# A two-layer graph network on one core: the ranks by the second sort digit as per-partition running counts on VectorE

## The chip, the cores and the metric

The kernel runs on one core of a Trainium2 chip (trn2). The time is device microseconds of one execution; lower is better. TensorE is called PE here, VectorE DVE, ScalarE ACT, GpSimd POOL and the queue of the sync engine SP, as in the profile.

## The reference, cut to what matters

```python
# x: 3125 x 256, 50000 edges (src, dst), sorted by dst before the kernel sees them
for i in range(3):                                     # layer 0, three hops
    msg = H[src] * edge_weight[:, None]
    Hn = segment_sum(msg, dst, 3125) @ Wn[i].T + bn[i]
    H = Hn + H @ Ws[i].T + bs[i]
    if i != 2: H = elu(H)
x = layernorm(x + H)
# layer 1: graph attention with 8 heads of 32 over the same edges
h = x @ W.T
alpha = leaky_relu(a_src.h[src] + a_dst.h[dst] + relu(edge_attr @ edge_W.T + edge_b).h[dst])
attn = softmax of alpha over the edges of each dst
out = layernorm(x + segment_sum(h[src] * attn, dst) + bias)
```

What counts here is how the edges are brought into order on the chip. The kernel doesn't use that they arrive sorted: it sorts records of 8 floats (source, destination, weight, three attributes, a flag) twice, once by pairs of node windows and once by destination.

## The kernel before, in words

The work goes through these stages, in order of time in the profiled execution.

**Ranks and scatter by pair, to about 559 us.** DVE and PE rank the 128 x 392 records by pair of windows, and POOL writes them to rows of memory, one indirect DMA for each of the 392 columns (line 608). SP reads the result back as `recs_pair`.

**Ranks by the low digit, on DVE and PE, in the shadow of that scatter.** The sort by destination is a radix sort with two digits of 64 values: the low six bits first, then the bits above. `digit_ranks(0)` (PE lines 753 to 778, DVE lines 1417 to 1470) computes the ranks. The 392 columns form 14 groups (`SEGS`) of 28 (`SEGC`). In a first pass DVE builds a one-hot of the digit for 7 groups at a time (128 x 448 bf16, line 1411) and PE sums all of them with a matrix of ones (line 757, 56 matmuls of 448 columns). DVE makes first ranks of the totals (lines 1426 to 1438, a scan of 896 elements and the starts of the digits) and PE loads them into two banks of PSUM as `seed` (line 762). In a second pass, for each of 28 columns and each half, DVE builds the one-hot again, PE adds the triangle of ones (`below_b`, line 770), DVE multiplies the bank by the one-hot and reduces (lines 1451 and 1454) to read the rank, and PE adds the rest of the ones (`rest_b`, line 776). Every fourth column DVE turns 56 ranks of each partition into row numbers in four small instructions (lines 1462 to 1468) and counts up `s_place`. Four slots of one-hots (`oh`) turn. Between these steps PE does the first products with the weights.

**Adjacency blocks, 573 to about 1100 us.** Steps of eight chunks build dense blocks of 128 x 256 of the weighted adjacency matrix and store them in memory. Meanwhile POOL scatters the records by the low digit (line 618) and reads them back to `rec` (line 627), at 1126 us.

**Three hops, 1105 to about 2128 us.** Hop `k` goes through 7 groups `g` of 512 node columns (the last has 53). In a group, PE starts with 8 records of line 915 and then, for each of 25 windows `w`, multiplies the loaded block `a_t` with two halves of the table (line 923, four records in the trace for two instructions). SP loads `a_t` ten ahead (lines 525 and 528). `behind` puts small products of the next hop after some windows (line 794), from `w` = 8 on; the first of them waits for `s_ht`, the ELU of the group before, which ACT and DVE make (DVE lines 1659 and 1663). The layer norm of the last hop and the projection follow in hop 2 in the same way.

**The second digit, inside hop `k` = 1.** `digit_ranks(1)` is run again by PE and DVE, cut into steps by generators. After each window of hop 1 PE issues the next of its rank steps, by the function `issued`: two a window for the first 28 windows (the counts), then one a window (seeds, `below_b` and `rest_b`), 172 steps in all:

```python
if k == 1:
    slot = g * USED + w
    for _ in range(issued(slot + 1) - issued(slot)):
        next(side)
```

DVE issues the steps that belong to a group's 25 windows (line 1651) ahead of that group's ELU. The DVE's pass is paced by PE's matmuls through `s_drd` and `s_pre`, and PE waits for DVE through `s_doh`, `s_dseed` and `s_pick`. As the places of four columns of all 14 groups are ready (56 DMAs), POOL scatters them to `rows_dst` (line 633, 392 indirect DMAs in all) and reads the sorted records back (line 638). `split_features` on DVE in the last group of hop 2 (line 1620) waits for that read.

**The attention layer, to the end.** POOL gathers the rows of `h` by edge (line 647, 416 indirect DMAs), PE and DVE compute the scores, and a second pass sums the messages.

The sort must keep the order of equal digits: the ranks of the second digit go over the columns first and over the partitions within a column, which is the order in which line 1468 with stride 392 laid out the records by the low digit (rank `r` in partition `r & 127`, column `r >> 7`).

Of the kernel before, what the change touches and what calls it, by code (L numbers as in the profile page):

```python
# [13 lines left out]
P = 128  # L14
# [42 lines left out]
HN = HS * DIG  # L57

# [18 lines left out]
assert USED <= 1 << WBITS and 4 * WBITS <= 24  # L77
assert EC % PIECE == 0 and PIECE % 4 == 0 and 0 < LAST < EC and EC % U == 0 and SEGS * SEGC == EC and SEGS % 2 == 0 and SEGC % MID == 0
# [4 lines left out]
def build(nc, x, src, dst, edge_attr, edge_weight, Wn, bn, Ws, bs, W, a_src, a_dst, edge_W, edge_b, bias, out):  # L83
    with ExitStack() as ctx:
# [63 lines left out]
        summed, q = carve(q, [DIG, SEGS])  # L148

# [93 lines left out]
        window_row = picked[0:1, :, :, :].rearrange("p b g s -> p (b g s)")[:, 0:2 * NC].rearrange("p (r c) -> p r c", r=2)  # L243
# [341 lines left out]
        def _(pool):  # L585
# [94 lines left out]
        SLOTS2 = SEGC  # L680
        RANK_OPS = 2 * SEGC + 2 + 4 * SEGC + 2

        def issued(slot):
            return min(2 * min(slot, SLOTS2) + max(0, slot - SLOTS2), RANK_OPS)

# [4 lines left out]
        def _(pe):  # L690
# [62 lines left out]
            def digit_ranks(q):  # L753
                n0 = 4 * SEGC * q
# [83 lines left out]
            for n, _ in enumerate(digit_ranks(0)):  # L838
# [63 lines left out]
            def hop(k, g):  # L902
# [14 lines left out]
                for w in range(USED):  # L917
# [347 lines left out]
        def _(dve):  # L1265
# [151 lines left out]
            def digit_ranks(q, stride, to, begins, d):  # L1417

                n0 = 4 * SEGC * q
                m0 = 2 * SEGC * q  # L1420
# [21 lines left out]
                for i in range(SEGC):  # L1442
# [14 lines left out]
                    if i % MID == MID - 1:  # L1457
                        j = i // MID
                        part = slice(i + 1 - MID, i + 1)
                        e = d + 16 + 3 * j  # L1460
                        dve.wait_ge(s_rk, m0 + 2 * i + 2)
                        v.tensor_copy(rk_i[:, 0, :, :], rk.rearrange("p (s i) -> p s i", s=SEGS)[:, :, part]).then_inc(s_dg, 1)
                        dve.wait_ge(s_dg, e + 1)
                        v.tensor_scalar(rk_i[:, 1, :, :], rk_i[:, 0, :, :], P - 1, None, ALU.bitwise_and).then_inc(s_dg, 1)
                        v.tensor_scalar(rk_i[:, 2, :, :], rk_i[:, 0, :, :], SHIFT, None,
                                        ALU.logical_shift_right).then_inc(s_dg, 1)
                        dve.wait_ge(s_dg, e + 3)
                        v.scalar_tensor_tensor(out=place[:, to, :].rearrange("p (s i) -> p s i", s=SEGS)[:, :, part],  # L1468
                                               in0=rk_i[:, 1, :, :], scalar=float(stride), in1=rk_i[:, 2, :, :],
# [3 lines left out]
            LOW_END = LOW0 + 16 + 3 * SEGC // MID  # L1473
# [35 lines left out]
            for _ in digit_ranks(0, EC, 1, low_begins, LOW0):  # L1509
# [84 lines left out]
            def dst_ranks():  # L1594
# [5 lines left out]
                yield from digit_ranks(1, NCD, 0, window_begins, DST0)  # L1600
                yield
                dve.wait_ge(s_ex, 1)
                v.tensor_copy(ex_col[:, :], bank[6][0:HI, 0:1]).then_inc(s_exc, 1)
                dve.wait_ge(s_exc, 1)
                v.tensor_scalar(started[:, :], iota_f[0:HI, 0:NC], ex_col[:, 0:1], None, ALU.is_ge).then_inc(s_exc, 1)
                yield
                dve.wait_ge(s_ex, 2)
                v.tensor_scalar(window_row[:, 0, :], bank[7][0:1, 0:NC], -1.0, None, ALU.add).then_inc(s_exc, 1)
                of = [window_row[:, 0, :].rearrange("p (g j) -> p j g", j=4)[:, j, :] for j in range(4)]
                word = window_row[:, 1, :].rearrange("p (j g) -> p j g", j=4)  # L1610
                for j, (high, low, to) in enumerate(((of[3], of[2], word[:, 0, :]), (word[:, 0, :], of[1], word[:, 1, :]),
                                                     (word[:, 1, :], of[0], quad_windows[:, :]))):
                    dve.wait_ge(s_exc, j + 3)
                    v.scalar_tensor_tensor(out=to, in0=high, scalar=float(1 << WBITS), in1=low, op0=ALU.mult,
                                           op1=ALU.add).then_inc(s_exc, 1)
# [27 lines left out]
            for k in range(HOPS):  # L1643
                for g in range(NG):
# [4 lines left out]
                    if k == 1:  # L1649
                        for _ in range(issued((g + 1) * USED) - issued(g * USED)):  # L1650
                            next(side)
                        if g == NG - 1:
                            next(side, None)
# [294 lines left out]
```

## Time and profile before

| | us |
|---|---|
| Median of 3 runs | 3014.15 (3014.09 to 3016.46) |
| The profiled execution, its own time | 3018.76 |
| Its span in the trace | 3016.7 |
| PE busy (share of the span) | 2460.3 (82%) |
| POOL busy | 1855.6 (62%) |
| DVE busy | 1722.3 (57%) |
| ACT busy | 1073.7 (36%) |
| Mean granted TensorE clock | 0.923 |

Shares of busy time are means over stages with different limits. Here each stage is bounded by another engine, so the stretch that the change touches has to be read by itself. A matmul in fp32 shows as two records in the trace.

### The profile page before, as it was taken

To read this page: it belongs to the slowest core of one execution; us is meant where nothing else is said; L and a number is where in the kernel's file an instruction comes from. 1 tells how busy PE (TensorE), PEld (TensorE's weight loads), DVE (VectorE), ACT (ScalarE), POOL (GpSimd) and SP (SyncE) were. 2 spreads that over 40 slices of the span, in tenths; PEclk is the share of its full clock that TensorE was granted. 3 is DMA by queue.
4 is the path that set the end of the run, shared out by engine and by line. 5 is a ranking of instruction groups with operands and counts; after the bars stand their busy time and mean duration, and the time that the engine had idled before them with its cause. 6 is when DMAs were issued, how large, how long until landed. Compare 5 with 4: busy or idle time off the path is not lost.

```text
span 3016.7 us, 48565 instructions
## 1 busy us (share of the span) xinstructions
PE 2460.3 (82%) x9398; PEld 1569.3 (52%) x9399; DVE 1722.3 (57%) x4280; ACT 1073.7 (36%) x3018; POOL 1855.6 (62%) x1739
## 2 busy tenths in 40 slices
PE   6999976477777779999899999999776767738883
PEld 5888853255555544445444454445554545525552
DVE  7765558799999940001334411103777777766667
ACT  1222221398888840000000000000333333338773
POOL 4777777777777770000057777770577777757774
PEclk9999979699999999999999999999788888869997
DMA  4000000255555565443344444543477777747772
GB/s 128 3 4 3 3 25 3 99 183 183 184 184 184 184 196 152 129 132 110 101 122 121 128 115 128 143 134 106 141 217 218 218 217 218 217 132 230 215 212 85
DMA packets 425652, 415.45 MB, mean 138 GB/s; under 512 B 85386, under 2 KB 411489, under 8 KB 424929
## 3 DMA queue, kind: packets, MB, share of 16 engines
q1 hardware_dynamic: 367681, 348.28, 36.9%
q0 software_dynamic: 57888, 66.23, 9.4%
q8 instruction: 32, 0.52, 0.1%
q14 instruction: 51, 0.42, 0.0%
HBM read 247.08 MB, written 167.17 MB: 137 GB/s over the span
## 4 chain that ended last, share of the span: by engine, by line
PE 37%; POOL 23%; issue 15%; SPq 10%; DVE 6%; DMA 4%; DVEq 3%; ACT 1%; ACTq 0%; POOLq 0%
PE psum L923 27%; POOL rows_by_pair L608 13%; POOL gath L647 10%; SPq L497 7%; PE psum L1039 2%; PE psum L915 2%; DMA gath<-gat_rows,rec 2%; SPq L491 2%; PE psum L794 1%; DMA adjacency<-merged 1%; PE psum L883 1%; PE psum L853 1%; DVE acc L1848 1%; DVEq L414 1%; DVE x L1848 1%
## 5 line engine op out<-in xcount | busy, mean ns | idle before, releaser
L633 POOL DMA_INDIRECT rows_by_dst<-rec,place x392 | 382.6, 976 | 534.0 <-DVE place L1468 405.9
L923 PE MATMUL psum<-a_t,acc 128*128 128x512 f32 (+1 forms) x1400 | 553.7, 551 | 0.0
L647 POOL DMA_INDIRECT gath<-gat_rows,rec x416 | 404.6, 973 | 213.0 <-issue 117.1
L618 POOL DMA_INDIRECT rows_by_low_digit<-rec,place x392 | 437.6, 1116 | 127.7 <-issue 127.7
L853 PE MATMUL psum<-rhot,lw 128*128 128x256 f32 x1440 | 381.8, 419 | 162.7 <-ACT lw L1110 124.3
L608 POOL DMA_INDIRECT rows_by_pair<-rec,place x392 | 389.0, 992 | 159.5 <-issue 126.7
L853 PEld LDWEIGHTS psum<-rhot,lw 128*128 128x128 f32 x1440 | 276.4, 206 | 268.1 <-ACT lw L1110 170.7
L923 PEld LDWEIGHTS psum<-a_t,acc 128*128 128x128 f32 x1400 | 257.3, 195 | 272.1 <-issue 268.3
L1576 DVE SCALAR_TENSOR_TENSOR merged<-merged,same_of,psum 128x256 f32<-128x256 f32 x720 | 309.7, 476 | 30.4 <-PE psum L853 18.7
L923 PE MATMUL psum<-a_t,x 128*128 128x512 f32 (+1 forms) x700 | 294.3, 549 | 0.0
L1110 ACT ACTIVATE lw<-lhot,recs_pair 128x128 f32<-128x128 bf16 x720 | 236.8, 387 | 98.6 <-DVE lhot L1559 87.8
L994 PE MATMUL psum<-x,acc 128*128 x832 | 258.5, 458 | 5.1 <-DVE acc L1715 4.4
L1039 PE MATMUL psum<-ht 128*128 128x264 f32 x832 | 214.2, 402 | 48.8 <-DVE acc L1848 45.2
L663 POOL TENSOR_TENSOR ht<-gath,digits 128x1024 f32<-128x1024 f32 x104 | 198.7, 1914 | 64.9 <-PE psum L1039 56.8
L1039 PEld LDWEIGHTS psum<-ht 128*128 128x128 f32 x832 | 151.1, 191 | 111.9 <-DVE acc L1848 86.0
L735 PEld LDWEIGHTS psum<-table,ohhiT 32*128 32x128 f32 x784 | 181.1, 318 | 53.2 <-issue 33.7
L994 PEld LDWEIGHTS psum<-x,acc 128*128 128x128 f32 x832 | 180.0, 231 | 50.6 <-issue 16.9
L735 PE MATMUL psum<-table,ohhiT 32*128 32x16 f32 x784 | 202.2, 375 | 1.4 <-issue 1.2
L1659 DVE TENSOR_SCALAR et<-et 128x512 f32<-128x512 f32 (+1 forms) x28 | 11.0, 394 | 334.0 <-ACT et L1138 333.8
L1715 DVE TENSOR_TENSOR acc<-wT,psum 128x528 f32<-128x528 f32 x208 | 145.2, 698 | 94.7 <-issue 41.8
L923 PEld LDWEIGHTS psum<-a_t,x 128*128 128x128 f32 x700 | 126.2, 191 | 114.0 <-issue 109.0
L1345 DVE SCALAR_TENSOR_TENSOR terms<-psum,kst,earlier 128x128 f32<-128x128 f32 (+1 forms) x392 | 139.8, 412 | 44.8 <-PE psum L720 34.3
(322 smaller groups left out, 3392.9 us busy)
## 6 DMA issues: line engine op xcount, KB each, us to landing
a_t<-adjacency SPq DMA_DIRECT2D x450, 256.0 KB, 2.7
adjacency<-merged SPq DMA_DIRECT2D x721, 128.0 KB
gat_h_by_edge<-gath SPq DMA_DIRECT2D x104, 528.0 KB, 4.2
gath<-gat_h_by_edge SPq DMA_DIRECT2D x104, 528.0 KB, 3.9
gath<-gat_rows,rec POOLq DMA_INDIRECT x416
rows_by_pair<-rec,place POOLq DMA_INDIRECT x392
rows_by_low_digit<-rec,place POOLq DMA_INDIRECT x392
rows_by_dst<-rec,place POOLq DMA_INDIRECT x392
```

Of the source, the lines that this page charges most:

```text
L497: sp.dma_start(adj[bass.ds(to[j], 1), :, :].rearrange("b p c -> p (b c)"), merged[:, j, :]).then_inc(s_st[j], 16)
L608: pool.indirect_dma_start(out=rows_pair, in_=rec[:, c, :], out_offset=bass.IndirectOffsetOnAxis(ap=place[:, 0, c:c + 1], axis=0), in_offse ...
L618: pool.indirect_dma_start(out=rows_low, in_=rec[:, c, :], out_offset=bass.IndirectOffsetOnAxis(ap=place[:, 1, c:c + 1], axis=0), in_offset ...
L633: pool.indirect_dma_start(out=rows_dst, in_=rec[:, c, :], out_offset=bass.IndirectOffsetOnAxis(ap=place[:, 0, c:c + 1], axis=0), in_offset ...
L647: pool.indirect_dma_start(out=gath[:, g % 4, c % 4, :], out_offset=None, in_=hh_dram, in_offset=bass.IndirectOffsetOnAxis(ap=rec_i[:, c, 0 ...
L735: pe.matmul(bank[7 * s][:, j * LO:(j + 1) * LO], ohhiT[:, 4 * s + j, :], table[:, half, :], start=True, stop=True, skip_group_check=True). ...
L853: pe.matmul(bank[j % 4][:, 0:SW], lw[:, p, j, :], rhot[:, p, j, :], start=True, stop=True).then_inc(s_bmm, 1)
L923: i = pe.matmul(sums[b], table_g[:, w, b * P:(b + 1) * P], a_t[:, q % NA, 0:width(g)], start=False, stop=w == USED - 1)
L994: i = pe.matmul(bank[4 + j][:, 0:HX], ohT[:, q % 2, j * P:(j + 1) * P], x0[:, bass.ds(ws[4 * (q % 2) + j], 1), :].rearrange("p c k -> p (c ...
L1039: pe.matmul(bank[4 * (q % 2) + j][:, 0:HX], onehot[:, q // 2, 4 * (q % 2) + j, :], val[:, q, j, :], start=True, stop=True).then_inc(s_mm, 1)
L1110: nc.scalar.activation(lw[:, p, j, :], lhot[:, p, j, :], ACT.Copy, scale=recs_pair[:, bass.ds(at, 1), 2]).then_inc(s_lw, 1)
L1576: v.scalar_tensor_tensor(out=merged[:, j, :], in0=merged[:, (j - 2) % U, :], scalar=same_of[:, bass.ds(s, 1)], in1=bank[j % 4][:, 0:SW], o ...
```

## The change

The layout of the records by the low digit is another one, and the ranks by the second digit are computed in another way. The 392 columns now form 7 groups (`RUNS`) of 56 (`RUN`). The order of the records goes over the groups, then the partitions, then the columns in a group: rank `r` lies in run `r // 56`, partition `run & 127`, group `run >> 7`. For that the low digit's row number takes nine small DVE instructions for every four columns instead of four.

For the second digit DVE counts the one-hots of each partition by itself: a bf16 sum (`counts`) over the 56 columns of all 7 groups at once. PE then runs two matmuls on these counts, one with ones (totals) and one with `below_b` (the partitions below). DVE keeps the next rank of each digit in `first` (128 x 448 fp32): a step multiplies it by the one-hot, adds the one-hot to it, and reduces the product to the ranks. PE has three side steps left in hop 1, at window 0 of groups 1, 2 and 3. DVE issues 55, 21, 20 and 16 steps ahead of the ELUs of groups 0 to 3, and none after. The window starts (lines 1603 to 1614) are computed inside the third and fourth of these parts. POOL scatters in batches of 28 DMAs in place of 56; there are 392 as before. The seeds, the 56 count matmuls, the 56 `below_b` and the 56 `rest_b` matmuls of the second digit are gone; those of the low digit stay.

```diff
+RUNS = HS
+RUN = EC // RUNS
...
+        first = seed[:, 0, :, :]
+        counts = seed[:, 1, :, :].rearrange("p s d -> p (s d)")[:, 0:HN // 2].bitcast(BF16).rearrange("p (s d) -> p s d", d=DIG)
...
-            for j in range(SEGC // MID):
+            for j in range(RUN // MID):
                 pool.wait_ge(s_place, SEGC // MID + j + 1)
                 for i in range(MID):
-                    for s in range(SEGS):
-                        c = s * SEGC + j * MID + i
+                    for s in range(RUNS):
+                        c = s * RUN + j * MID + i
...
+        RANK_STEPS = [RUN - 1, 1 + 20, 20, RUN - 40, 0, 0, 0]
...
             def dst_windows():
-                yield from digit_ranks(1)
+                pe.wait_ge(s_drd, 4 * SEGC + RUN - 1)
+                pe.matmul(bank[6][:, 0:HN], ones_b[:, :], flat(counts), start=True, stop=True).then_inc(s_pre, 1)
+                pe.matmul(bank[7][:, 0:HN], below_b[:, :], flat(counts), start=True, stop=True).then_inc(s_pre, 1)
+                yield
+                pe.wait_ge(s_dseed, 3)
                 pe.transpose(bank[6][0:HI, 0:P], begin[:, 2, HI:2 * HI], identf[:, :]).then_inc(s_ex, 1)
...
-                    if k == 1:
-                        slot = g * USED + w
-                        for _ in range(issued(slot + 1) - issued(slot)):
-                            next(side)
+                    if k == 1 and w == 0 and g in (1, 2, 3):
+                        next(side)
...
+                        v.tensor_scalar(eighth, rank_, 3, None, ALU.logical_shift_right).then_inc(s_dg, 1)
...
+                        v.tensor_scalar(run_, eighth, 0.5, 8.0 / RUN, ALU.add, ALU.mult).then_inc(s_dg, 1)
...
+                        v.scalar_tensor_tensor(out=eighth, in0=run_, scalar=RUN / 8.0, in1=eighth, op0=ALU.mult,
+                                               op1=ALU.is_gt).then_inc(s_dg, 1)
...
+                onehot_of(0, counts)
+                onehot_of(1, oh[:, 1, :, :])
+                for i in range(1, RUN):
+                    if i + 1 < RUN:
+                        if i >= 4:
+                            dve.wait_ge(s_drd, used + i - 3)
+                        onehot_of(i + 1, oh[:, (i + 1) % 4, :, :])
+                    dve.wait_ge(s_doh, built + i + 1)
+                    if i > 1:
+                        dve.wait_ge(s_drd, used + i - 1)
+                    v.tensor_tensor(counts, counts, oh[:, i % 4, :, :], ALU.add).then_inc(s_drd, 1)
+                    yield
...
+                v.tensor_tensor_scan(flat(run_sums), flat(run_keep), flat(run_totals), 0.0, ALU.mult, ALU.add).then_inc(s_dg, 1)
...
+                v.tensor_tensor(first, first, bank[7][:, 0:HN].rearrange("p (s d) -> p s d", d=DIG), ALU.add).then_inc(s_dseed, 1)
...
+                    v.tensor_tensor(picked[:, i % 2, :, :], first, oh[:, i % 4, :, :], ALU.mult).then_inc(s_pick, 1)
+                    dve.wait_ge(s_pick, picks + i + 1)
+                    v.tensor_tensor(first, first, oh[:, i % 4, :, :], ALU.add).then_inc(s_drd, 1)
+                    v.tensor_reduce(rk.rearrange("p (s i) -> p s i", s=RUNS)[:, :, i], picked[:, i % 2, :, :], X,
+                                    ALU.add).then_inc(s_rk, 1)
...
                     if k == 1:
-                        for _ in range(issued((g + 1) * USED) - issued(g * USED)):
+                        for _ in range(RANK_STEPS[g]):
                             next(side)
```

## Rows read from the trace of the kernel before

**Rows 1.** The page, chain that ended last: shares of the span by line.
```profile
PE psum L923 27%; POOL rows_by_pair L608 13%; POOL gath L647 10%; SPq L497 7%; PE psum L1039 2%; PE psum L915 2%; DMA gath<-gat_rows,rec 2%; SPq L491 2%; PE psum L794 1%; DMA adjacency<-merged 1%; PE psum L883 1%; PE psum L853 1%; DVE acc L1848 1%; DVEq L414 1%; DVE x L1848 1%
```

**Rows 2.** Windows of hop 0, hop 1 and its group 1: busy times, clock, DMA.
```profile
1105.00:1418.60 313.60, 313.51 (x853) 154.56 (x854) 13.10 (x26) 23.48 (x48) 15.06 (x16) 0.99 0.47 137
1418.60:1775.10 356.50, 348.56 (x1033) 172.07 (x1032) 136.46 (x305) 24.76 (x53) 182.77 (x187) 0.99 0.42 115
...
1475.30:1541.90 66.60, 58.66 (x156) 27.64 (x155) 29.10 (x61) 3.72 (x9) 7.03 (x7) 0.92 0.35 99
```

**Rows 3.** The chain in order of time, starts of groups: start us, us, what.
```profile
1303.55 3.43 PE psum L915 x8
...
1353.35 3.43 PE psum L915 x8
1356.79 15.45 PE psum L923 x36
...
1418.61 3.50 PE psum L915 x8
...
1475.34 3.43 PE psum L915 x8
...
1541.95 3.43 PE psum L915 x8
1596.48 3.43 PE psum L915 x8
...
1775.11 3.50 PE psum L915 x8
...
1822.39 3.43 PE psum L915 x8
```

**Rows 4.** Groups of instructions in hop 1, forms kept apart.
```profile
L633 POOL DMA_INDIRECT rows_by_dst<-rec,place x188 | 183.8, 978 | 465.6 <-DVE place L1468 405.9 <-issue 59.7
...
L1411 DVE TENSOR_TENSOR digits<-digits,iota_b 128x448 bf16<-128x448 bf16 x112 | 38.5, 386 | 34.3 <-PE psum L757 34.2
```

**Rows 5.** Timeline of hop 1: first one-hots, then the seeds.
```profile
1420.97 1.30 DVE L1411 TENSOR_TENSOR digits<-digits,iota_b 128x448 bf16<-128x448 bf16 x4
...
1485.10 1.70 DVE L1426 COPY digits<-psum 128x448 f32<-128x448 f32 x2 [3.69 <-PE psum L757]
...
1494.71 1.86 PE L762 MATMUL psum<-digits,identf 128*128 128x448 f32 x2 [7.94 <-DVE digits L1438]
...
1496.37 3.26 PE L923 MATMUL psum<-a_t,x 128*128 128x512 f32 x4
```

**Rows 6.** Timeline of DVE, low digit's second pass and the wait behind it.
```profile
461.06 0.61 DVE L1451 TENSOR_TENSOR digits<-psum,digits 128x448 f32<-128x448 f32 x1
461.71 0.62 DVE L1454 TENSOR_REDUCE digits<-digits 128x7 f32<-128x448 f32 x1
462.25 0.68 DVE L1411 TENSOR_TENSOR digits<-digits,iota_b 128x448 bf16<-128x448 bf16 x2
...
479.58 0.19 DVE L1462 CAST digits<-digits 128x56 int32<-128x56 f32 x1
...
480.26 0.69 DVE L1411 TENSOR_TENSOR digits<-digits,iota_b 128x448 bf16<-128x448 bf16 x2
...
569.35 0.81 DVE L1545 TENSOR_SCALAR low_i<-recs_pair 128x720 int32<-128x720 int32 x1 [10.27 <-DMA recs_pair<-rows_by_pair]
```

**Rows 7.** Timeline of DVE, the ELU of group 1 of hop 1.
```profile
1542.52 0.43 DVE L1659 TENSOR_SCALAR et<-et 128x512 f32<-128x512 f32 x1 [3.06 <-ACT et L1138]
...
1544.26 1.29 DVE L1663 SCALAR_TENSOR_TENSOR ht<-zt,et 128x512 f32<-128x512 f32 x2 [0.73 <-ACT zt L1140]
```

**Rows 8.** Timeline, second scatter: its start, its read-back, and its reader.
```profile
1532.91 1.21 POOL L633 DMA_INDIRECT rows_by_dst<-rec,place  x1 [405.89 <-DVE place L1468]
...
2046.11 0.57 POOL L638 DMA_DIRECT2D rec<-rows_by_dst  x1 [2.52 <-DMA rows_by_dst<-rec,place]
...
2102.97 1.05 DVE L1620 COPY digits<-rec 128x1728 f32<-128x1728 f32 x1
```

More of the change, by code:

```diff
@@ L837, in _ @@
             products = first_products()
-            for n, _ in enumerate(digit_ranks(0)):
+            for n, _ in enumerate(digit_ranks()):
                 if n % 3 == 2:
@@ L1459, in digit_ranks @@
                         part = slice(i + 1 - MID, i + 1)
-                        e = d + 16 + 3 * j
+                        e = d + 16 + 8 * j
+                        rank_, eighth, run_ = (rk_i[:, a, :, :] for a in range(3))
                         dve.wait_ge(s_rk, m0 + 2 * i + 2)
-                        v.tensor_copy(rk_i[:, 0, :, :], rk.rearrange("p (s i) -> p s i", s=SEGS)[:, :, part]).then_inc(s_dg, 1)
+                        v.tensor_copy(rank_, rk.rearrange("p (s i) -> p s i", s=SEGS)[:, :, part]).then_inc(s_dg, 1)
@@ new lines, in digit_ranks @@
+                        dve.wait_ge(s_dg, e + 4)
+                        v.scalar_tensor_tensor(out=run_, in0=eighth, scalar=-1.0, in1=run_, op0=ALU.mult,
+                                               op1=ALU.add).then_inc(s_dg, 1)
+                        dve.wait_ge(s_dg, e + 5)
+                        v.tensor_scalar(eighth, run_, P - 1, None, ALU.bitwise_and).then_inc(s_dg, 1)
+                        dve.wait_ge(s_dg, e + 6)
+                        v.tensor_scalar(run_, run_, SHIFT, None, ALU.logical_shift_right).then_inc(s_dg, 1)
@@ L1470, in digit_ranks @@
+                        v.scalar_tensor_tensor(out=rank_, in0=eighth, scalar=float(EC - RUN), in1=rank_, op0=ALU.mult,
+                                               op1=ALU.add).then_inc(s_dg, 1)
+                        dve.wait_ge(s_dg, e + 8)
+                        v.scalar_tensor_tensor(out=place[:, 1, :].rearrange("p (s i) -> p s i", s=SEGS)[:, :, part],
+                                               in0=run_, scalar=float(RUN - P * RUN), in1=rank_,
                                                op0=ALU.mult, op1=ALU.add).then_inc(s_place, 1)
@@ L1609, in dst_ranks @@
[L1609 to L1615, printed above, removed]
+                built, used, picks, ranked = 4 * SEGC, 4 * SEGC, 2 * SEGC, 2 * SEGC
@@ new lines, in dst_ranks, with onehot_of @@
+                by_run = digit.rearrange("p (s i) k -> p s i k", s=RUNS)
+                def onehot_of(i, out):
+                    v.tensor_tensor(out.rearrange("p s (a b) -> p s a b", b=2),
+                                    by_run[:, :, i, :].unsqueeze(2).broadcast_to([P, RUNS, DIG // 2, 2]),
+                                    pairs_of(iota_b[:, 0:DIG]).unsqueeze(1).broadcast_to([P, RUNS, DIG // 2, 2]),
+                                    ALU.is_equal).then_inc(s_doh, 1)
+                onehot_of(0, counts)
@@ new lines, in window_words @@
+                def window_words():
+                    dve.wait_ge(s_ex, 2)
+                    v.tensor_scalar(window_row[:, 0, :], bank[7][0:1, 0:NC], -1.0, None, ALU.add).then_inc(s_exc, 1)
+                    of = [window_row[:, 0, :].rearrange("p (g j) -> p j g", j=4)[:, j, :] for j in range(4)]
+                    word = window_row[:, 1, :].rearrange("p (j g) -> p j g", j=4)
+                    for j, (high, low, to) in enumerate(((of[3], of[2], word[:, 0, :]), (word[:, 0, :], of[1], word[:, 1, :]),
+                                                         (word[:, 1, :], of[0], quad_windows[:, :]))):
+                        dve.wait_ge(s_exc, j + 3)
+                        v.scalar_tensor_tensor(out=to, in0=high, scalar=float(1 << WBITS), in1=low, op0=ALU.mult,
+                                               op1=ALU.add).then_inc(s_exc, 1)
```

91 lines of the change are left out of this document (64 added, 27 removed).

## The prediction, made before the changed kernel was run

> **What bounds the kernel now.** I read the chain by line first [rows 1]: the hops' matmuls (line 923) are its largest part with 27% of the span, and no line of the digit ranks is among its large ones. So DVE, busy 57% of the span, is not what to count. Then the windows of the hops [rows 2]: in hop 1, where the second digit is ranked, PE is busy 348.6 of 356.5 us, and DVE only 136.5; hop 0, the same work without ranks, takes 313.6. The difference, 42.9 us, is about what can be had there. Third, the chain in order of time [rows 3], whose steps at line 915 are the starts of groups. A group without rank steps takes 1353.35 - 1303.55 = 49.80 us; hop 1's group 2, with 25 of them, 1596.48 - 1541.95 = 54.53. PE is the bound in both, so each matmul taken from it counts in full: (54.53 - 49.80)/25 = 0.189 us.
>
> **What PE loses.** Group 0 of hop 1 holds 50 rank matmuls: 1475.34 - 1418.61 = 56.73 us, against 1822.39 - 1775.11 = 47.28 for group 0 of hop 2 [rows 3]; 9.45/50 is 0.189 again. The 56 counts, 56 `below_b` and 56 `rest_b` make 168 x 0.189 = 31.8 us. Group 1 took 66.61, that is 16.81 over 49.80. It holds 28 rank steps, 26 of them such matmuls (4.9 us); the other 11.9 are the seeds. There PE stood 7.94 us for DVE's first ranks, and the first four records behind it took 3.26 us where nine windows' 36 take 15.45 (1.72 for four) [rows 3, 5]. The granted clock of the group was 0.92 where the hop has 0.99 [rows 2]: after the idle stretch PE ran for a while at the lower of its levels, 1.2 instead of 2.4 GHz. In the new code the seeds are not loaded into PSUM and PE goes on with the hop while DVE makes them, so wait, seeds and slow stretch go together. Added are two matmuls of 448 columns, 2 x 0.189 = 0.4; transpose and window count stay. Sum: 31.8 + 11.9 - 0.4 = 43.3 us, near the 42.9 of the other route.
>
> **Does DVE keep up?** Now PE waits for DVE at few places, and each needs its time. *Counts:* DVE starts at 1420.97 [rows 5], four one-hots there take 1.30 us, 0.30 from start to start. The bf16 add has no row; from below it costs as the one-hot, 0.30, from above as an fp32 instruction over 448, 0.54 (461.71 to 462.25, [rows 6]). It has the one-hot's types and shape, so I take 0.34 for each: 55 x 0.68 = 37 us, done at 1459. Even 55 x (0.34 + 0.54) ends at 1470. PE asks after the first window of group 1: 1418.61 + 47.28 + 3.43 + 1.72 = 1471.0. No wait; what covers these 37 us is group 0's 47.
>
> *Seeds:* from 1485.10 to 1494.71, 9.6 us, over 896 elements [rows 5]. Now 448; about 1.7 of it is small window arithmetic that stays, the rest halves, and one add of 0.6 from PSUM comes: 6.3. PE needs them at group 2, so they end at 1471.4 + 6.3 = 1477.7.
>
> *A rank step:* one-hot 0.34, product 0.65 to the start of what waits for it, reduction 0.54 [rows 6]; new is the fp32 add to `first`, bounded by 0.30 and 0.66, taken as 0.54 like the reduction of the same length. Four small instructions close every fourth step, 480.26 - 479.58 and 0.12 of wait, 0.8 us, 0.20 a step. Together 2.27, and 2.6 if every instruction waits out the one before. Twenty steps take 45.4. The ELU takes 1542.52 to 1545.55, 3.0 with its waits [rows 7]; 2.2 of it are DVE's four instructions, and with ACT done early only these stand. So the ELU of group 1 is ready at 1477.7 + 0.3 + 45.4 + 2.2 = 1525.6; PE asks for it after window 8 of group 2, at 1465.9 + 49.8 + 0.4 + 3.43 + 9 x 1.72 = 1535.0. The next: 1525.6 + 45.4 + 0.6 for the window starts + 2.2 = 1573.8 against 1584.8. The last 16 steps end at 1612, before group 3 does. The slack is 9 and 11 us, so I cost DVE's step at nothing. It is used up from 2.74 us a step in the first part, 2.54 in the second.
>
> *Low digit:* nine small instructions instead of four at seven places. 35 x 0.22 = 7.7 us more on DVE, in front of the buckets; behind them DVE waited 10.27 us for `recs_pair`, which POOL's scatter sets [rows 6]. Nothing again, with 2.6 us to spare; if each costs 0.43, 15 us come and 5 show.
>
> *POOL and SP:* the number of DMAs is unchanged, 392 each. The first batch is ready four steps behind the seeds, at 1487, 46 us earlier than 1532.91. The scatter took 2046.11 - 1532.91 = 513 us, so it ends at 2000; its reader, at 2102.97, moves to 2060 [rows 8]. The slack stays near 57 us, and batches of 28 DMAs are ready every 9 us, long ahead of their 36. The loads of `a_t` kept up with group 0 of hop 2, 47.28 us beside the same scatter, so they should with hop 1. The records by the low digit land in other rows of memory: neighbours 32 bytes apart where they were 12.5 KB. No row prices that. The stores of adjacency blocks beside that scatter are 1% of the chain, 30 us [rows 1]; a tenth of that either way is 3, and I take 0.
>
> **Sum.** The profiled execution: 3016.7 - 43.3 = 2973.4 us of span, 2975.5 of its own 3018.76. The median of the runs is 4.6 below that execution, so 3014.15 - 43.3 = 2970.9. About 0.2% (6 us) is what a measurement of this kernel can tell from no change.
>
> **Rivals.** *A: DVE's parts overrun their groups.* At 2.8 us a step, the ELU of group 2 would be 11 us late, and with a slow stretch behind the wait like the one in group 1 about 15 are given back: 2986. For it: three instructions over 448 elements in a step where there were two, waits on the neighbour between them, and the slack of 9 us is all there is. Against: every piece but the add has a row, and 2.6 gives only some 3 us: 2974 to 2976.
>
> *B: the low digit's extra instructions outlast the 10.27 us.* Above: 2976.
>
> *C, the slower one: DVE is held up by POOL.* From hop 1's group 1 on, the scatter runs beside the rank steps, and POOL's DMA instructions read their row numbers from SBUF. The Trainium skill (SBUF — State Buffer, on the shared port pair) says that a VectorE instruction with two SBUF inputs and a GpSimd one that reads SBUF exclude each other, and the second to issue waits for the whole of the first. The product now reads SBUF twice, where it read PSUM, and the add to `first` does too. POOL's instruction has a mean of 978 ns [rows 4]. If product and add waited one out each, a step would take 2.27 + 1.94 = 4.2 us. Past 2.64 the 56 steps decide: the delay is 56 x (step - 2.64), which eats the 43 us at 3.41 and is 87 at 4.2: 2971 + 87 = 3058. Against it, and that decides for me: the one-hot reads SBUF twice as well, and in hop 1, about half of them beside the scatter, 112 take 38.5 us, 0.34 each; the first four, before any scatter, take 1.30, 0.33 each [rows 4, 5].
>
> *D: the matmuls' place is taken by something hidden behind PE*, as the loads of `a_t`: then hop 1 stays near 356 us and the time near 3010. Against: group 0 of hop 2.
>
> **How the numbers follow.** Forecast 0.78, with 2965 to 2977 of its own (the unpriced scatter, 2.6 us a step, the runs' own spread of 2.4). A 0.12, mostly 2977 to 2990. B 0.02, D 0.04, C 0.04. Faster by more than 0.2%: 0.78 + 0.12 + 0.02 = 0.92; D is the same, C slower. The range 2964 to 2986 leaves out D, C, and the upper part of A, with some of the forecast's edges: under 2 in 10.
>
> **What would show it.** In the new trace hop 1's groups 1 to 4 should each take 49.8 to 50.2 us and group 0 47.3; no wait of PE for DVE in hop 1 and a granted clock of 0.99 or 1.00 in group 1; count steps of 0.68 us, rank steps of 2.2 to 2.3; POOL's first DMA of the second scatter near 1487; DVE's wait for `recs_pair` near 2.6 us. A wait of line 794 for the ELU would be A. One-hots, products or adds of well over 0.7 us beside the scatter would be C. I am wrong if hop 1 doesn't fall to about 313 us, or if it does and the stages before and after it don't keep their lengths.

## The result, and the profile after

The changed kernel takes 2981.82 us (median of 4 runs, 2979.59 to 2982.78) against 3014.97 us in the runs beside it: a ratio of 0.9888, 95% interval 0.9871 to 0.9906. It is faster, by 33 us. The time is inside the predicted range and 10.9 us above the forecast of 2970.9. The profiled execution took 2980.92 us, its span 2979.1.

The page, chain that ended last, shares by line:

```profile
PE psum L933 27%; POOL gath L657 10%; SPq L507 7%; PE psum L741 6%; PE psum L1047 4%; PE psum L726 3%; DMA gath<-gat_rows,rec 3%; PE psum L925 2%; PE psum L804 2%; SPq L501 2%; PE psum L717 1%; DMA adjacency<-merged 1%; DVE digits L1458 1%; DVE acc L1947 1%; PE psum L745 1%
```

Line 933 is line 923 of before [rows 1], still with 27%. POOL's scatter by pair (line 608, 13% in [rows 1]) has left the chain, and PE's lines 741, 726 and 717 and DVE's low digit (line 1458) have come in for it: in the changed kernel the low digit outlasts the scatter and its read-back. The windows of hop 0, hop 1 and its group 1 answer to [rows 2]:

```profile
1106.30:1419.50 313.20, 313.18 (x853) 154.38 (x854) 13.07 (x25) 23.49 (x48) 14.12 (x15) 0.99 0.47 137
1419.50:1732.70 313.20, 313.20 (x863) 154.38 (x862) 177.04 (x444) 24.76 (x53) 185.09 (x182) 1.00 0.47 131
1466.80:1517.00 50.20, 50.20 (x127) 23.77 (x127) 45.34 (x107) 3.91 (x8) 22.23 (x21) 1.00 0.47 133
```

Hop 1 fell from 356.5 to 313.2 us, 43.3 as forecast. PE is busy in all of it, at a granted clock of 1.00, and DVE has gone from 136 to 177 us. The chain in order of time, starts of groups of hop 1 (line 925), beside [rows 3]:

```profile
1419.52 3.50 PE psum L925 x8
1466.80 3.43 PE psum L925 x8
1516.98 3.43 PE psum L925 x8
1566.89 3.43 PE psum L925 x8
1617.68 3.43 PE psum L925 x8
1667.48 3.43 PE psum L925 x8
```

Groups of 47.28, 50.18, 49.91, 50.79 and 49.80 us. Only group 3 is outside the forecast's 49.8 to 50.2, by 0.6; its side step of two small matmuls (line 795) lies in it. The timeline of DVE in hop 1, a rank step (product, add, reduction, and the one-hot of the next), answers to [rows 5, 6], and the ELU of group 1, with PE's first product that needs it, to [rows 7]:

```profile
1479.78 0.62 DVE L1698 TENSOR_TENSOR digits<-digits 128x448 f32<-128x448 f32 x1
1480.43 0.62 DVE L1700 TENSOR_TENSOR digits<-digits 128x448 f32<-128x448 f32 x1
1480.97 0.61 DVE L1701 TENSOR_REDUCE digits<-digits 128x7 f32<-128x448 f32 x1
1481.50 0.38 DVE L1626 TENSOR_TENSOR digits<-digits,iota_b 128x448 bf16<-128x448 bf16 x1
1481.80 0.62 DVE L1698 TENSOR_TENSOR digits<-digits 128x448 f32<-128x448 f32 x1
...
1523.64 0.82 DVE L1758 TENSOR_SCALAR et<-et 128x512 f32<-128x512 f32 x2
1524.57 1.29 DVE L1762 SCALAR_TENSOR_TENSOR ht<-zt,et 128x512 f32<-128x512 f32 x2
...
1535.81 1.03 PE L804 MATMUL psum<-wT,ht 128*128 128x256 f32 x4
```

A step takes 1481.80 - 1479.78 = 2.02 us. The ELU is done at 1525.86 and PE asks for it at 1535.81, so DVE is 9.9 us ahead. In the groups of instructions of hop 1 the sums over all steps are seen, beside [rows 4]:

```profile
L1626 DVE TENSOR_TENSOR digits<-digits,iota_b 128x448 bf16<-128x448 bf16 x112 | 42.7, 384 | 0.1
L1700 DVE TENSOR_TENSOR digits<-digits 128x448 f32<-128x448 f32 x56 | 35.0, 625 | 1.9
L1698 DVE TENSOR_TENSOR digits<-digits 128x448 f32<-128x448 f32 x56 | 34.6, 618 | 0.0
```

Two places lost time. DVE's timeline at the end of the low digit, a batch of nine small instructions (562.89 is its last), and what follows, beside [rows 6]:

```profile
560.99 0.23 DVE L1470 CAST digits<-digits 128x56 int32<-128x56 f32 x1
561.25 0.19 DVE L1472 TENSOR_SCALAR digits<-digits 128x56 int32<-128x56 int32 x1
...
562.89 0.22 DVE L1488 SCALAR_TENSOR_TENSOR place<-digits 128x56 int32<-128x56 int32 x1
563.02 0.96 DVE L1534 COPY bucket<-psum 128x360 f32<-128x360 f32 x2
...
570.13 0.79 DVE L1565 TENSOR_SCALAR low_i<-recs_pair 128x720 int32<-128x720 int32 x1
```

SP's issue of the read-back, and its time to landing:

```profile
L497 SPq DMA_DIRECT2D recs_pair<-rows_by_pair x1: 349/349/349, 557.2 to 557.2; - x1
```

```profile
recs_pair<-rows_by_pair SPq DMA_DIRECT2D x1, 2880.0 KB, 9.9
```

The batch takes 2.03 us, where the kernel before has 0.68 [rows 6]. The low digit ended at 563.0, against 551.9, and DVE waits for `recs_pair` no more. The data had landed at 557.2 + 9.9 = 567.1, and DVE took it at 570.1: it comes 3.0 us late itself. In the profile before the data landed 2.2 us later, at 569.3, because POOL's scatter ended later there; so only 0.8 of the 3.0 are seen when the two profiles are laid side by side. And the last loop, in which DVE adds the messages, runs from the load of `cin` to the end in 2979.1 - 2642.7 = 336.4 us; before, in 3016.7 - 2684.9 = 331.8.

The two profiled spans can be added up: hop 0 starts 1.2 us later (1106.32, against 1105.09), hop 1 is 43.3 shorter, the last loop 4.6 longer: 37.5 of the 37.6 between the spans.

### The profile page after: what moved, and what is told of

Same layout as the page of the kernel before. It is cut to its first block, busy times and chain, and to the rows that moved or that the text cites. A ratio compares the mean times of both kernels' runs of the same rounds, so it can differ in the third digit from the quotient of the medians.

```text
span 2979.1 us, 48453 instructions
## 1 busy us (share of the span) xinstructions
PE 2430.0 (82%) x9228; PEld 1554.3 (52%) x9229; DVE 1774.0 (60%) x4454; ACT 1073.3 (36%) x3018; POOL 1860.2 (62%) x1739
## 4 chain that ended last, share of the span: by engine, by line
PE 51%; issue 11%; SPq 10%; POOL 10%; DVE 8%; DMA 6%; DVEq 2%; ACT 1%; ACTq 0%; POOLq 0%
PE psum L933 27%; POOL gath L657 10%; SPq L507 7%; PE psum L741 6%; PE psum L1047 4%; PE psum L726 3%; DMA gath<-gat_rows,rec 3%; PE psum L925 2%; PE psum L804 2%; SPq L501 2%; PE psum L717 1%; DMA adjacency<-merged 1%; DVE digits L1458 1%; DVE acc L1947 1%; PE psum L745 1%
## 5 line engine op out<-in xcount | busy, mean ns | idle before, releaser
L643 POOL DMA_INDIRECT rows_by_dst<-rec,place x392 | 389.2, 993 | 491.9 <-DVE place L1713 362.3
L933 PE MATMUL psum<-a_t,x 128*128 128x512 f32 (+1 forms) x700 | 274.2, 547 | 0.0
L1353 DVE SCALAR_TENSOR_TENSOR terms<-psum,kst,earlier 128x128 f32<-128x128 f32 (+1 forms) x392 | 139.9, 412 | 44.6 <-PE psum L726 34.1
```

Of the source, the lines that this page charges most:

```text
L643: pool.indirect_dma_start(out=rows_dst, in_=rec[:, c, :], out_offset=bass.IndirectOffsetOnAxis(ap=place[:, 0, c:c + 1], axis=0), in_offset ...
L933: i = pe.matmul(sums[b], table_g[:, w, b * P:(b + 1) * P], a_t[:, q % NA, 0:width(g)], start=False, stop=w == USED - 1)
```

## The experiments

Each run has a kernel before beside it on the same chip. Five of them (e1 to e5) fell on two chips on which every kernel of this case took about 4250 us, with many more and longer waits on all engines in the stretches where POOL issues its indirect DMAs; of those only what the text says is used.

**The kernels repeated (e1, e2).** No edit.

> The kernel before, unchanged, for a second trace of it. The hop gave the predicted 43.3 us in the traces, but the medians differ by 33.2 only. Theory P (part of the gap is that the profiled execution of before was a slow one): this trace has a span near 3013, with the scatter by pair ending near 556.4 us as in the changed kernel, not at 558.5. Theory A (the last loop of the attention layer got slower with the change, whichever execution one looks at): a period of 10.10 us for four groups here again. Rival R (the period varies from run to run): 10.1 or 10.3 by chance.

> The changed kernel, unchanged, for a second trace. Theory A: the last loop of the attention layer has 10.31 us for four groups again, and the stretch from the last load of the carries to the end is about 336 us. Rival R: it may have 10.10. Time 2982 by both.

Measured: e1 4260.57 us, e2 4263.26, with 4264.66 beside them (ratios 0.9994, 0.9983 to 1.0004, and 1.0002, 0.9992 to 1.0011). The windows of hop 1 in e1 and in e2:

```profile
2121.40:2831.90 710.50, 393.02 (x1033) 190.57 (x1032) 135.48 (x305) 24.67 (x53) 382.73 (x393) 0.76 0.23 62
```

```profile
2121.20:2837.70 716.50, 408.06 (x863) 172.35 (x863) 178.49 (x444) 24.62 (x53) 387.87 (x393) 0.68 0.22 61
```

PE is busy in little over half of hop 1, and 170 records of matmuls fewer (863, 1033 before) shorten nothing: the change is worth its 43 us only where PE is the bound. What it does show is the last loop. From its first add to its last, e1 takes 260.8 us and e2 265.2; the profiles of before and of the changed kernel have 260.7 and 265.2. So the 4.5 us there belong to the program, not to the one execution. Theory P can't be read from e1, but it can from e7 and e11, whose code up to hop 1 is that of the kernel before: their read-back of `recs_pair` is issued at 557.2 and 557.8 us, not at 559.5, and their hop 0 starts at 1102.4 and 1103.7, not at 1105.1. The profiled execution of the kernel before was late there, by 1.4 to 2.7 us.

**The seeds asked for later, in the kernel before (e3, e5, e7).** The late steps are issued six windows later; nothing moves to DVE:

```diff
-            return min(2 * min(slot, SLOTS2) + max(0, slot - SLOTS2), RANK_OPS)
+            return min(2 * min(slot, SLOTS2) + max(0, slot - SLOTS2 - 6), RANK_OPS)
```

> The kernel before, but PE issues six windows of the hop without a rank step between the last count and the seeds. All 168 rank matmuls stay. My account of the 43.3 us puts 31.8 on the matmuls and 11.9 on the wait for the seeds and the slow clock behind it: then group 1 of hop 1 falls from 66.6 to about 56.5 us, there is no wait for the seeds and the time is about 10 us below before, 3005. Rival (the time lost in group 1 is DVE's, and comes back later as a wait for its steps): group 1 gets shorter but groups 2 to 5 longer, and the time stays at 3015.

> The same kernel as in e3, since in the runs e1 to e4 all kernels took 4260 us, with long waits of every engine that the trace puts down to no work of the kernel, and so could not tell terms of 10 us apart. Should this set be like the first measurement (before at 3015): by my account (31.8 us for the matmuls, 11.9 for the wait for the seeds and the slow clock behind it) group 1 of hop 1 falls from 66.6 to about 56.5 us and the time is 3005. Rival (what PE wins in group 1 comes back as a wait for DVE's steps): groups 2 to 5 get longer and the time stays at 3015. Since nothing else differs from before, the trace is also a second one of it: by theory P (the profiled execution of before was a slow one outside the hops) the scatter by pair ends near 556.4 us and not at 558.5; by theory A (the last loop got slower with the change, not by chance) it has a period of 10.10 us for four groups.

> The kernel before with its forty-two rank matmuls spread one a slot from six slots later, so that each of the first group's seeds is asked for later against the counts that feed it, and no count is moved to VectorE. My account of the change (theory M, matmuls and seed waits are separate terms): the 11.9 us that group 1 of hop 1 loses in the kernel before (66.60 us against the 54.7 that its matmuls ask for) come back to about half or more, since they are waits and the slow clock behind them, and groups 2 to 5 of hop 1 keep their lengths: hop 1 takes 345 to 351 us in place of 356.5, and the time is 3003 to 3009 us. Rival theory W (the 11.9 us are work of group 1 that is done in any order): hop 1 stays at 356 us and the time at 3014 to 3016.

Measured: e3 4245.82 us (0.9967, 0.9951 to 0.9984) and e5 4242.87 (0.998, 0.9962 to 0.9997), on the two chips named above; their waits beside POOL's DMAs leave open where it comes from. The one to read is e7: 3016.62 us, median of ten runs, against 3014.93 (0.9995, 0.9982 to 1.0009). No gain, where theory M expected 3003 to 3009, yet the chain in order of time has it:

```profile
1415.86 3.50 PE psum L915 x8
...
1472.60 3.43 PE psum L915 x8
...
1482.31 10.30 PE psum L923 x24
...
1495.19 0.75 PE psum L762 x2
...
1527.68 3.43 PE psum L915 x8
...
1746.33 1.03 PE psum L915 x8
...
1773.99 4.66 PE psum L915 x8
```

Group 1 takes 1527.68 - 1472.60 = 55.1 us in place of 66.6 [rows 2, 3]: the 11.5 us of wait and slow clock are gone, and the seeds' matmuls (line 762) take 0.75 for two where one pair took 1.86 behind the wait [rows 5]. But group 6, which has 53 columns, takes 27.7 us instead of 15.45. The windows of groups 5 and 6 in e7:

```profile
1691.30:1746.30 55.00, 55.00 (x151) 25.58 (x150) 22.32 (x49) 4.46 (x10) 41.83 (x43) 1.00 0.33 86
1746.30:1774.00 27.70, 27.70 (x126) 26.27 (x126) 3.63 (x8) 3.19 (x7) 21.14 (x22) 0.55 0.33 82
```

The granted clock is 0.55, nearly all of the group at the lower level, 1.2 GHz, though PE had not idled in the group before (55.0 of 55.0 us busy, clock 1.00). The 12.2 us lost there eat the 11.5 won in group 1, and hop 1 takes 358.1 us where theory M expected 345 to 351; without the slow group it would be 345.9. Why the clock fell here is not shown. The ten runs fall in two sets, three at 3004.47 to 3006.75 us and seven at 3014.77 to 3019.66; the profiled one is of the seven. The three stand where theory M puts them (3003 to 3009), and the gap is the size of the slow group. That the three had no slow group is the natural reading; they weren't profiled.

**One matmul more for every window of hop 0 (e9).** It adds 175 matmuls to the changed kernel:

```diff
+                    if k == 0:
+                        pe.matmul(bank[6][:, 0:HN], ones_b[:, :], ew_j[:, :, :].rearrange("p a d -> p (a d)")[:, 0:HN],
+                                  start=True, stop=True)
```

> The changed kernel with one 448-column matmul more after each of hop 0's 175 windows, whose result nobody reads. Theory M (TensorE sets the pace of a hop, so a matmul counts in full at 0.189 us): 175 x 0.189 = 33.1 us, hop 0 takes 346 us in place of 313 and the time is 3015 us; a further gain or loss of up to 5 us would come from the last loop, if its 10.31 us per four groups hangs on how many instructions TensorE's program has ahead of it (theory Q), in which case it would be 10.10 here. Rival theory G (matmuls fill gaps that the one-hots and semaphores leave): hop 0 grows by less than half of 33 us, under 2999 us.

Measured: 3008.88 us (0.9982, 0.9972 to 0.9993), 27.1 over the changed kernel. The windows of its hop 0 and of group 1 of it:

```profile
1103.80:1448.80 345.00, 345.00 (x1028) 172.04 (x1029) 13.07 (x25) 23.69 (x49) 14.11 (x15) 0.99 0.43 126
...
1157.20:1211.80 54.60, 54.60 (x151) 26.03 (x150) 2.15 (x4) 3.98 (x9) 0.00 (x0) 1.00 0.42 121
```

A full group grows from 49.80 to 54.53 us (starts of groups in the chain), 0.189 a matmul, the price of the prediction to the last digit. The hop grows by 31.8, not 33.1: in group 6 the 25 cost 3.4 and not 4.7. Theory M holds for the hop, though 3008.88 is under its 3015: in the profile hop 0 starts 2.5 us earlier than in the changed kernel's, and the stretch from hop 2 to the load of `cin` is 2.7 shorter, with the same code. Other profiles of that code scatter as much. The last loop stays at 10.3 us per four groups, so theory Q, that it hangs on PE's program, finds no support; e10 and e11 below settle it.

**Two reductions more in each rank step (e12).** In the changed kernel:

```diff
+                    v.tensor_reduce(more_t[:, 0, :], iota_f[:, 0:HN].rearrange("p (s d) -> p s d", d=DIG), X, ALU.add).then_inc(s_more[0], 1)
...
+                    v.tensor_reduce(more_t[:, 1, :], iota_f[:, 0:HN].rearrange("p (s d) -> p s d", d=DIG), X, ALU.add).then_inc(s_more[1], 1)
```

> The changed kernel with two reductions of 448 elements more in each of the 56 rank steps on VectorE, 0.54 us each, whose result nobody reads. A step takes 2.21 us now and would take 3.29. Theory S (TensorE's own matmuls set hop 1, VectorE has slack up to about 2.64 us a step, and beyond it each tenth of a microsecond counts 56 times): hop 1 grows from 313 to 349 us, the exponential units of groups 1 to 5 come late and TensorE waits for VectorE, 36 to 42 us more: 3018 to 3024 us. Rival theory T (DMA or the one-hots, not VectorE, stand next in line, or VectorE's slack is wider than I think): less than 15 us more. By theory F the last loop, which starts at instruction 2960 here, takes 10.10 us per four groups, which takes 4.6 us off.

Measured: 3015.92 us, 34.1 over the changed kernel. Its hop 1, and in it the group of instructions that waits for the ELU (line 806):

```profile
1418.40:1766.80 348.40, 320.24 (x863) 157.18 (x863) 235.66 (x556) 24.74 (x53) 209.24 (x204) 0.96 0.43 118
```

```profile
L806 PE MATMUL psum<-wT,ht 128*128 128x256 f32 x100 | 28.5, 410 | 28.2 <-DVE ht L1770 28.2
```

Four steps with their batch take 1502.03 - 1489.12 = 12.9 us, 3.23 a step. PE waited three times, 28.2 us, each time for the ELU; the other 7.0 of the 35.2 us that the hop grew are PE's own matmuls at the lower clock behind the waits (clock 0.96, PE busy 320.2 us in place of 313.2). By the prediction's threshold, 56 x (3.23 - 2.64) = 33. This is rival A of the prediction, forced by the edit, and with 2.2 us a step the change stays inside the slack. Theory S holds: the hop takes 348.4 us for its 349, though the time is 2 us under its 3018 to 3024. What theory F expected here failed: the last loop took 10.30 us per four groups (see below).

**The floor of the low digit as one multiply-add (e4, e8).** Five small instructions a batch in place of nine; the conversion to int32 rounds to nearest here, so `r/56 + 0.5/56 - 0.5` gives the floor:

```diff
-                        v.tensor_copy(rank_, rk.rearrange("p (s i) -> p s i", s=SEGS)[:, :, part]).then_inc(s_dg, 1)
...
-                        v.tensor_scalar(eighth, rank_, 3, None, ALU.logical_shift_right).then_inc(s_dg, 1)
...
-                        v.tensor_scalar(run_, eighth, 0.5, 8.0 / RUN, ALU.add, ALU.mult).then_inc(s_dg, 1)
...
-                        v.scalar_tensor_tensor(out=eighth, in0=run_, scalar=RUN / 8.0, in1=eighth, op0=ALU.mult,
-                                               op1=ALU.is_gt).then_inc(s_dg, 1)
...
-                        v.scalar_tensor_tensor(out=run_, in0=eighth, scalar=-1.0, in1=run_, op0=ALU.mult,
-                                               op1=ALU.add).then_inc(s_dg, 1)
...
+                        v.tensor_scalar(run_, ranks_, 1.0 / RUN, 0.5 / RUN - 0.5, ALU.mult, ALU.add).then_inc(s_dg, 1)
```

> The changed kernel with the run number of the low digit's ranks made by one multiply-add that rounds to an integer, so four small instructions fewer at each of the seven places (five instead of nine). Theory L (the low digit's new arithmetic outlasts the wait for recs_pair): DVE ends it 6 to 7 us earlier, at about 556, waits for recs_pair again, and the time is 2 to 3 us lower, 2979. Rival (it was hidden all the same): the stretch to the first adjacency block is as long as before and the time 2982. The number of DVE instructions ahead of the last loop changes by 28 plus their waits, so theory A allows the last loop another period; if it goes to 10.10 the time falls by 5 us more.

> The changed kernel with the low digit's floor as one multiply-add rounded by the conversion, five small operations a batch in place of nine. Theory B (the nine small operations outlast what they lie beside, and this shows): they fell at 2.1 to 2.25 us a batch, some 0.24 each, so four fewer in 14 batches give 14 x 4 x 0.2 = about 11 us back, the low digit ends near 552 in place of 563, the read of the paired records is again waited for, and what follows starts 2 to 3 us earlier: 2978 to 2980 us. Rival theory H (the low digit was hidden all the same, what follows waits for POOL's scatter): 2981 to 2983 us, no change. By both the last loop keeps its 10.3 us per four groups.

Measured: e4 4266.65 us (1.0009, 1.0 to 1.0018), on one of the chips named above, open. e8: 2977.08 us (0.9872, 0.9855 to 0.9888), 4.7 under the changed kernel. DVE's timeline in e8:

```profile
553.06 0.22 DVE L1471 TENSOR_SCALAR digits<-digits 128x56 int32<-128x56 f32 x1
...
554.03 0.96 DVE L1525 COPY bucket<-psum 128x360 f32<-128x360 f32 x2
...
566.70 0.92 DVE L1556 TENSOR_SCALAR low_i<-recs_pair 128x720 int32<-128x720 int32 x1 [5.49 <-DMA recs_pair<-rows_by_pair]
```

The low digit ends 9.0 us earlier, 1.3 for each of its 7 batches (the expectation miscounted them as 14). DVE waits for `recs_pair` again, and reads it 3.4 us earlier. By the trace theory B holds; the time alone would not show it, as 4.7 us between sessions is no more than the intervals of the two ratios allow. The wait is 5.49 and not 10.27 us for two reasons: the data landed 2.6 us earlier than in the profile before, and the five instructions end the low digit 2.1 later than the old four. In e7 and e11, which have the kernel before's low digit, DVE waited 7.27 and 7.34 us: the 10.27 were one execution's.

**A pad in front of the last loop (e6).** Twelve `nop` instructions on DVE between hops 1 and 2 of the changed kernel.

> The changed kernel with twelve empty instructions (NOPs) on DVE in the first group of hop 2, where DVE waits anyway. Of the 43.3 us that hop 1 gave in the traces, 5 were lost in the last loop of the attention layer, whose four groups took 10.31 us instead of 10.10. Theory A (the loop's period hangs on where it stands in DVE's program, 228 instructions further on than in before): with the pad it stands 240 further, a multiple of 16, and the period is 10.10 again, the time 5 us lower, 2977. Rival R (chance, or something in the data's place in memory): the period stays at 10.31, or varies from run to run without regard to the pad. Should the kernels take 4260 us again, only the period of that loop counts.

Measured: 2979.25 us, two runs (0.9878, 0.985 to 0.9907); the last loop 10.3 us per four groups, no change. It told nothing on the theory: the instructions aren't in the program that ran, and the trace has 10457 records of DVE with them in the source and without. It is one more measurement of the changed kernel.

**A pad that stays (e10, e11).** Waits on a value long reached; two become one instruction (64 and 200 records more in the traces). In e10, with e8's floor, 128 of them; in e11, in the kernel before, 400:

```diff
+                    if k == HOPS - 1 and g == 0:
+                        for i in range(128):
+                            dve.wait_ge(s_ht, NG * (HOPS - 2) + 1 + i % 2)
```

> The changed kernel with the floor of run e8, and 128 waits on a value long reached, which compile to 64 instructions, in VectorE's program between hops 1 and 2, where VectorE is idle. Theory F (the last loop's 10.31 us per four groups in place of 10.10 come from where its 113 instructions lie in VectorE's program: in the changed kernel and in e8 one add is late at the same instruction, number 2875 of the program, though in another group of the loop, and the first instruction behind the jump back is 0.1 us later than in the kernel before): with the loop starting at instruction 2884 and not 2848 or 2820 nothing lies on that place, the loop takes 10.10 us per four groups, and the time is 4 to 5 us under e8's, 2972 to 2973 us. Rival theory K (the period comes from something else that the change alters): the loop stays at 10.31, and the time at 2977 us.

> The kernel before with 400 waits on a value long reached, which compile to 200 instructions, in VectorE's program between hops 1 and 2, so that its last loop starts at instruction 2820 in place of 2620, as in e8. Theory F: the kernel before now has the slow loop too, 10.31 us per four groups in place of 10.10, one add late in the second group of the loop, and the time is 4 to 5 us longer, 3019 us. Theory K: 10.10 us, and 3015 us.

Measured: e10 2973.59 us (0.9858, 0.9842 to 0.9875), 3.5 under e8; e11 3021.56 (1.0016, 1.0007 to 1.0026), 5.4 over the kernel before: theory F had named 2972 to 2973 and 3019. DVE's timeline in the last loop of the changed kernel: the end of a turn (four groups), the first instruction behind the jump back (line 1953), and the next group's adds (line 1947):

```profile
2819.73 0.42 DVE L1947 TENSOR_TENSOR x<-x,psum 128x264 f32 x1
2820.34 0.18 DVE L1953 TENSOR_REDUCE ht<-digits 128x32 f32 x1 [0.18 <-issue]
...
2822.28 0.42 DVE L1947 TENSOR_TENSOR acc<-acc,psum 128x264 f32 x1
2822.67 0.43 DVE L1947 TENSOR_TENSOR x<-x,psum 128x264 f32 x1
```

The same place in e10 (its lines 1941 and 1947):

```profile
2814.43 0.42 DVE L1941 TENSOR_TENSOR x<-x,psum 128x264 f32 x1
2814.93 0.19 DVE L1947 TENSOR_REDUCE ht<-digits 128x32 f32 x1
...
2816.85 0.42 DVE L1941 TENSOR_TENSOR acc<-acc,psum 128x264 f32 x1
2817.19 0.42 DVE L1941 TENSOR_TENSOR x<-x,psum 128x264 f32 x1
```

And e11, where it is the second group whose last add is late:

```profile
2860.20 0.42 DVE L1851 TENSOR_TENSOR x<-x,psum 128x264 f32 x1
2860.80 0.19 DVE L1857 TENSOR_REDUCE ht<-digits 128x32 f32 x1 [0.18 <-issue]
...
2865.21 0.42 DVE L1851 TENSOR_TENSOR acc<-acc,psum 128x264 f32 x1
2865.61 0.43 DVE L1851 TENSOR_TENSOR x<-x,psum 128x264 f32 x1
```

Behind the jump back the changed kernel loses 0.61 us from the start of the add to that of the reduction, e10 0.50; the last add of the group comes 0.39 us behind the one before it, in e10 0.34. With what follows from both, a turn takes 10.3 us against 10.10, and there are 26 turns. From first add to last: 265.2 us changed, 259.9 in e10, 265.5 in e11, 260.7 before. The same code, 5 us more or less by its place alone: theory F holds in both runs, and K falls. Counted in the compiled program of DVE, the late add is number 2875 where the loop begins at 2848 (changed, first group) and where it begins at 2820 (e8 and e11, second group). The traces don't show these numbers, but their distances: from the kernel before to the changed one 228 records of DVE more lie ahead of the loop, 200 in e8 and e11, 264 in e10, 340 in e12, and a turn has 113.

e12 tells what F had wrong. Its loop begins at 2960, past that place, and has a late add too, the first of the second group (1.23 us behind the reduction, 1.11 in the others), number 3003: 128 instructions on. A boundary every 128 instructions fits every trace: 2875 or 3003 lies inside the loop of 113 where it begins at 2848, 2820 or 2960, and no such place lies in 2620 to 2732 (before, e7) or 2884 to 2996 (e10). That it is the fetching of instructions is argued from this, not shown.

## Why the prediction was right, and by how much it was off

**Right.** The bound, the price of a matmul (0.189, again in e9), the 31.8 us of matmuls and the 11.9 of wait, seeds and slow clock: hop 1 fell by the 43.3 summed. e7 parts the second term from the first: group 1 alone gave back 11.5 with all rank matmuls in place.

**DVE keeps up,** near each figure. Counts 0.61 us a step (forecast 0.68). The seeds' arithmetic took 1479.17 - 1472.24 = 6.9 us (6.3). A rank step is 2.02, with its share of the batch 2.21 (2.27): the fp32 add to `first` costs 0.54 from start to start, as taken. ELU of group 1 done at 1525.86 (1525.6), 9.9 us before PE asks for it (9); that of group 2 at 1572.62 (1573.8), 14.0 before (11). First DMA of the second scatter at 1488.7 (1487), its end 2006 (2000). Rival A was not met, and e12 shows that it does come when the steps are longer.

**Rival C was wrong.** With POOL's scatter beside them product and add have means of 0.618 and 0.625 us, the one-hot 0.384 as before [rows 4], though product and add read SBUF twice. POOL's instructions of the scatter have a mean of 993 ns over all 392, against 976 before. The rule of the Trainium skill (SBUF — State Buffer, on the shared port pair) that a VectorE instruction with two SBUF inputs and a GpSimd one that reads SBUF exclude each other doesn't show against POOL's indirect DMAs; a POOL instruction that computes was not tried.

**Low digit: the term was mis-sized, and its cover too.** "35 x 0.22 = 7.7 us more on DVE ... Nothing again, with 2.6 us to spare": the seven batches of nine small instructions take 1.89 to 2.23 us, 2.05 on average, where the old ones have 0.68 to 0.92, 0.77 on average, so 1.28 more a batch and 9.0 in all. The low digit ended 11.1 us later than in the profile before; the ends in other profiles of the same two codes lie 8.9 to 10.3 apart. The 10.27 us of wait, taken from one profile, were 7.3 in e7 and e11. So DVE takes `recs_pair` late: 3.0 us behind its landing in the changed kernel's profile, 3.3, 3.6 and 1.0 in e6, e9 and e12, and 0.0 in e8 and e10 with five instructions. That is rival B, which had 0.02, in its small form.

**The step that failed** is the one that took the untouched stages to keep their lengths; the prediction names it only at the end, as a sign of being wrong ("the stages before and after it don't keep their lengths"). The last loop lost 4.6 us by the place at which its unchanged instructions came to lie, 228 further on. e10 gets them back.

**The remainder.** Between the forecast gain, 43.3 us, and the gain in medians, 33.2, are 10 us. The last loop is 4.6 of them and the low digit 1 to 3.6. What is left, 2 to 4.5 us, is not located, and no more than sessions differ by: the same changed program gained 33.2 and 36.4 (e6) us. The forecast also took the distance of the profiled execution from the median, 4.6, as fixed; the changed kernel's profiled execution lay 0.9 below its own median, and the kernel before's was late in the scatter by pair. e10, with both repairs, gains 42.6 us over the runs beside it (38 to 48 by its interval), which is the forecast's 43.3 within the noise. So the two named losses account for the gap as far as these runs can tell. It is the best version: 2973.59 us, against 3016.20 beside it.

## What to carry to other kernels

When an engine is busy in all of a stretch, price its instruction by the difference of two groups that differ only in how many they have; the gain is then the count times that price, as long as what takes over the work keeps ahead of each hand-over, not only of the total. An idle stretch of PE can cost more than its own length, through the clock behind it (here 7.9 us of wait and 11.9 in all with the seeds); but taking it out gains only if no slow stretch comes elsewhere, so read the group lengths after the change and not the repaired place alone. A wait that one profile shows is that execution's slack: the 10.27 us here were 7.3 in two others, and they were the cover of a term put at nothing. And a few hundred instructions more ahead of a tight loop cost it 2% here: compare the cadence of loops that nobody touched.

## What the runs showed that was not expected

- **A loop's place in its engine's program.** 10.1 or 10.3 us for a turn of 113 DVE instructions, 260 or 265 us in all, by its place, at five places.
- **A clock that falls without an idle stretch.** In e7 TensorE went to 1.2 GHz for a group of 53-column matmuls right behind 55 us of full work at 1.00, and the group took 27.7 in place of 15.45 us; in the profiles of before and e11 the same group ran at full clock. Group 6 of hop 2 is no such case, since PE has idle time there: in every profile near 3000 us the clock is at 0.50 for 27 to 31 us at its end, before (0.56 over 2100 to 2128 us) and after (0.53 over 2058 to 2086) alike, so it takes no part in the comparison.
- **Two chips on which the stretches with POOL's indirect DMAs are longer.** There the stretches with scatters or gathers took longer, hop 1 of the kernel before 710 us in place of 356, while hop 0, without them, took its 313 us. Not explained here.
